# Issuing the two shift-row matmuls behind a pair's second units in a windowed-attention kernel

## Chip, cores and metric

The kernel runs on one core of one Trainium2 chip. The metric is the device time of one execution in microseconds (us). Engines are named as in the profile: PE (TensorE, matmuls), DVE (VectorE), ACT (ScalarE), POOL (GpSimd), SP (the queue that issues the DMAs).

## Reference: what is computed

A group normalisation (32 groups over 384 channels, per image) is followed by shifted window attention with a residual, on 16 images of 56 x 56 tokens. Cut to what matters:

```
x = x + attention(group_norm(x))
# attention: roll by (-3, -3); qkv = x @ w_qkv.T; windows of 7 x 7 = 49 tokens, 12 heads of 32
dots = q @ k.T * 32 ** -0.5 + pos_emb[relative index] + shift masks (last window row, last window column)
out = softmax(dots) @ v; out = out @ w_out.T + b_out; roll back by (3, 3)
```

## Kernel before

**Tiling.** A row is a band of 7 image rows: 8 windows, 392 tokens. There are 128 rows (8 an image), and a row has four pairs of windows. The unit of work is a step: one pair, k = 0 to 7 within a tick of two rows, and p = k % 4 within the row, so steps p = 0, 1, 2, 3 repeat 128 times (512 steps). The four compute engines each run a hand-written instruction stream with a loop over images and, inside, four ticks of eight steps; they meet only at semaphores. Nothing reorders the work: an engine that waits holds up everything written behind it.

**Precision.** Each float32 operand is kept as a high and a low half-precision part, and a product takes three matmuls (high-high, high-low, low-high).

**What PE issues in step t**, in this order (function `step`, from line 1316): `transposed_scores(t - 1)`, `scores(t)`, `transpose_attended(t - 3)`, the first part of the step's units, `attend(t - 2)`, `shift_rows(t)`, the second part, `project_out(t)`, the third part.

**Units** prepare the next row while this one is attended. A q, k or v unit is nine matmuls of about 390 columns (`project_unit`, L1201 and L1205); an x unit transposes a third of the channels of a later row (`x_unit`, four matmuls, L1189). The table FILL spreads them over the four steps of a row:

```
FILL = [([("q", 0)], [("k", 0)], [("q", 1)]),
        ([("k", 1)], [("q", 2), ("x", 0)], [("k", 2), ("x", 1)]),
        ([("v", 0)], [("x", 2)], [("v", 1)]),
        ([("v", 2)], [], [("v", 3)])]
```

So the second part is k0 in step p = 0, q2 and x0 in p = 1, x2 in p = 2 and nothing in p = 3. All units of the program alternate between two PSUM banks (ps_pj): a unit may start when the unit two before it has been taken from its bank. A q, k or v unit is taken in two moves: ACT copies the high part (qk L686, vh L682), then DVE subtracts it for the low part (qk L973, vl L968), and only then is the bank free. An x unit is taken by DVE alone (xn L960).

**Shift rows.** `shift_rows` is two small matmuls (L1257) that turn the row maxima (mt, made by DVE: lg L1008, mx L1024, mw L1030, mt L1041 and L1045) into rows that shift the logits. ACT copies them (tq L762), POOL spreads them over the heads (rb L653), and PE's `transposed_scores` of the next step adds them (L1269). ACT's order in a step is fixed as well:

```
                    shift_rows(t)
...
                        probabilities_high(t - 1)
...
                        x_highs(tk, k)
                        units(tk, k, 1)
                        units(tk, k, 2)
```

That is: tq, then ph (two exponentials, L775), then the high parts of x, and then the high parts of the second and third units. DVE's order is logits, maxima, attended_low (atl L1019), low part of the first unit, `invert` and `normalize` (rv L1049, av L1054), low parts of the second units, the group statistics of a later image (L809), `output` (xb L1063), `split_probabilities` (pl L1069), low parts of the third units. POOL's is rb, its half of pl (L639), the low parts of x (xl L619), the residual (xb L627).

**Exceptions to the common row.** `project_out` (nine matmuls, L1310) has a chunk in steps p = 2, 3, 0 and in p = 1 of every sixteenth row only. The sixth row of an image (but the last) also makes the next image's statistics on DVE and PE (L1177), and the row before it measures more groups. The last image measures none. The last row has no units.

Of the kernel before, what the change touches and what calls it, by code (L numbers as in the profile page):

```python
# [109 lines left out]
def need(eng, sem, value):  # L110

    if isinstance(value, int) and value <= 0:
        return
    eng.wait_ge(sem, value)
# [70 lines left out]
def chunk_at(t):  # L185

    row, p = divmod(t, PAIRS)
    row, part = {2: (row - 1, 0), 3: (row - 1, 1), 0: (row - 2, 2), 1: (row - 2, CHUNKS)}[p]
    if not 0 <= row < ROWS or part == CHUNKS and row % SHARE != SHARE - 1:
        return None  # L190
    return row, part
# [6 lines left out]
def chunks_before(t):  # L198
    return sum(u < t for u in CHUNK_STEPS)
# [22 lines left out]
def step_units(tk, k):  # L222
    first, second, third = ([u for u in part if u[0] != "x" or not tk.last] for part in FILL[k % 4])
    return first, second, [("mean", 0)] * (k == 4 and tk.finishes) + [("var", 0)] * (k == 5 and tk.finishes) + third
# [10 lines left out]
def units_before(tk):  # L235
    return PRO_UNITS + tk.image * IMAGE_UNITS + sum(len(units_in(Tick(tk.image, part))) for part in range(tk.part))


def unit_at(tk, k, kind, i):
    return len(units_in(tk, range(k))) + units_in(tk, [k]).index((kind, i))  # L240
# [20 lines left out]
def build(nc, x, w_qkv, pos, w_out, b_out, const, y):  # L261
# [7 lines left out]
    with ctx:  # L269
# [877 lines left out]
        def _(pe):  # L1147
# [26 lines left out]
            def stat_unit(kind, unit, bank, fz):  # L1174
                bank_free(unit)
                pe.wait_ge(s_fz, fz)
                mm(ps_pj[bank][:, 0:GROUPS], const_of("mean_of", SP_), (red1 if kind == "mean" else red4)[:, :],  # L1177
                   start=True, stop=True).then_inc(s_pj, 1)
# [5 lines left out]
            def x_unit(unit, bank, b, c, loaded):  # L1184

                bank_free(unit)
                pe.wait_ge(s_load[b], loaded)
                for p in range(PAIRS):
                    m = nc.tensor.transpose(ps_pj[bank][:, p * PT:(p + 1) * PT], xs[:, b, p, c * 128:(c + 1) * 128],  # L1189
                                            perm_in[:, 1 if p == PAIRS - 1 else 0, :])  # L1190
                m.then_inc(s_pj, 1)

            def project_unit(unit, bank, kind, i, b, x_ready):
                bank_free(unit)
                pe.wait_ge(s_xh, x_ready)
                pe.wait_ge(s_xl, x_ready)
                for c in range(KC):
                    for n_, (xa, wa) in enumerate(((xh, wh), (xh, wl), (xl, wh))):
                        on = dict(start=c == 0 and n_ == 0, stop=c == KC - 1 and n_ == 2)
                        if kind == "v":  # L1200
                            m = mm(ps_pj[bank][:, 0:C], xa[:, b, c, 2 * i:2 * i + 2, :].rearrange("p w n -> p (w n)"),  # L1201
                                   wa[:, c, 2 * C:3 * C], **on)
                        else:
                            o = (C if kind == "k" else 0) + i * 128
                            m = mm(ps_pj[bank][:, 0:RT].rearrange("p (w n) -> p w n", w=NW), wa[:, c, o:o + 128],  # L1205
                                   xa[:, b, c, :, 0:N], **on)
                m.then_inc(s_pj, 1)
# [11 lines left out]
            def units(tk, k, part):  # L1219

                base, odd, n = units_before(tk), k // 4, tk.n
                for kind, i in step_units(tk, k)[part]:
                    j = unit_at(tk, k, kind, i)
                    if kind == "x":
                        x_unit(base + j + 1, j % 2, odd, i, LOADS * (n + 2))
                    elif kind in STAT_KINDS:
                        stat_unit(kind, base + j + 1, j % 2, FZ * (tk.image + 1) + (2 if kind == "mean" else FZ_MEAN))
                    else:
                        project_unit(base + j + 1, j % 2, kind, i, 1 - odd, 6 * n + 6 + 3 * odd)
# [12 lines left out]
            def scores(t, tk, k):  # L1242
                odd, p, n = k // 4, k % 4, tk.n
                if p == 0:
                    pe.wait_ge(s_stack[odd], STACK * (n + 1))
                need(pe, s_lg, t)
                need(pe, s_tc, t)
                for hh in range(2):
                    m = score_blocks(ps_sa, odd, p, hh, False, start=True, stop=True)
                m.then_inc(s_sa, 1)  # L1250

            def shift_rows(t):

                pe.wait_ge(s_ml, t + 1)
                need(pe, s_tc, t)
                for hh in range(2):
                    m = mm(rows_out[:, hh, :], mt[:, hh, :], eb[:, :], start=True, stop=True)  # L1257
                m.then_inc(s_tp, 1)

            def transposed_scores(t, tk, k):  # L1260

                odd, p = k // 4, k % 4
                pe.wait_ge(s_rb, t + 1)
                need(pe, s_ph, t)
                kind = bias_kind(tk, odd, p)
                for hh in range(2):
                    for w in range(2):
                        rows = slice(w * PAD, (w + 1) * PAD)
                        mm(ps_st[rows, hh, 0:HH * N], bt[:, kind, rows], rb[:, hh, :, :].rearrange("p h n -> p (h n)"),  # L1269
                           start=True, stop=False, skip_group_check=True)  # L1270
                for hh in range(2):
                    m = score_blocks(ps_st, odd, p, hh, True, start=False, stop=True, skip_group_check=True)
                m.then_inc(s_st, 1)
# [14 lines left out]
            def transpose_attended(t):  # L1288
                pe.wait_ge(s_av, t + 1)
                need(pe, s_fin, chunks_before(t + 3))  # L1290
                for c in range(KC):
                    m = nc.tensor.transpose(at_out[:, c, :],  # L1292
                                            av[:, 4 * c:4 * c + 4, :].rearrange("p h d -> p (h d)"), perm_out)
                m.then_inc(s_at, 1)

            def project_out(t):
                if not chunk_at(t):
                    return
                row, part = chunk_at(t)
                pe.wait_ge(s_al, min(t - 2, PAIRS * ROWS))  # L1300
                need(pe, s_fin, chunks_before(t))
                if part == CHUNKS:
                    pe.wait_ge(s_over, row + 1)
                for c in range(KC):
                    if part == CHUNKS:
                        high, low = overh[:, c, :], overl[:, c, :]
                    else:
                        high, low = (a[:, row % 2, c, part * 128:part * 128 + 128] for a in (ath, atl))
                    for n_, (a, w) in enumerate(((high, woh), (high, wol), (low, woh))):
                        m = mm(ps_post[:, 0:C], a, w[:, c, :], start=c == 0 and n_ == 0, stop=c == KC - 1 and n_ == 2)  # L1310
                m.then_inc(s_out, 1)

            def back(tk, k, lag):
                return (tk, k - lag) if k >= lag else (tk.back, k - lag + 8)

            def step(tk):
                for k in range(8):
                    t = 8 * tk.n + k
                    if not (tk.first and k < 1):
                        transposed_scores(t - 1, *back(tk, k, 1))  # L1320
                    scores(t, tk, k)
                    if not (tk.first and k < 3):
                        transpose_attended(t - 3)
                    if not (tk.last and k >= 4):
                        units(tk, k, 0)
                    if not (tk.first and k < 2):
                        attend(t - 2, *back(tk, k, 2))
                    shift_rows(t)
                    if not (tk.last and k >= 4):
                        units(tk, k, 1)  # L1330
                    project_out(t)
                    if not (tk.last and k >= 4):
                        units(tk, k, 2)

            def image(m):
                for part in range(PARTS):
                    step(Tick(m, part))
# [33 lines left out]
```

## Time and profile before

| | |
|---|---|
| time, median of 3 runs | 4250.94 us (4249.82 to 4251.36) |
| profiled execution: time, span | 4250.67 us, 4248.9 us |
| mean granted TensorE clock | 0.996 |
| PE busy | 3998.8 us (94%), 64304 matmuls |
| DVE, ACT, POOL busy | 3676.0 us (87%), 2313.5 us (54%), 2102.1 us (49%) |
| DMA | 131 GB/s on average, 16 engines 48.5% busy with the kernel's own queue |

Busy shares are averages over the whole span. Matmuls are pipelined, so PE at 94% is not PE at its peak, and the time between the starts of two neighbouring groups says more than the duration of one. The time not covered by work of an engine shows in the waits.

### The profile page before, as it was taken

To read this page: it belongs to the slowest core of one execution; us is meant where nothing else is said; L and a number is where in the kernel's file an instruction comes from. 1 tells how busy PE (TensorE), PEld (TensorE's weight loads), DVE (VectorE), ACT (ScalarE), POOL (GpSimd) and SP (SyncE) were. 2 spreads that over 40 slices of the span, in tenths; PEclk is the share of its full clock that TensorE was granted. 3 is DMA by queue.
4 is the path that set the end of the run, shared out by engine and by line. 5 is a ranking of instruction groups with operands and counts; after the bars stand their busy time and mean duration, and the time that the engine had idled before them with its cause. 6 is when DMAs were issued, how large, how long until landed. Compare 5 with 4: busy or idle time off the path is not lost.

```text
span 4248.9 us, 163876 instructions
## 1 busy us (share of the span) xinstructions
PE 3998.8 (94%) x64304; PEld 2757.0 (65%) x64304; DVE 3676.0 (87%) x9291; ACT 2313.5 (54%) x4609; POOL 2102.1 (49%) x1813
## 2 busy tenths in 40 slices
PE   3999999999999999999999999999999999999998
PEld 1666666666666666666666666666666666666665
DVE  6888888888888888888888888888888888888886
ACT  0555555555555555555555555555555555555554
POOL 1445545544554545554455455545545455554554
PEclk9999999999999999999999999999999999999998
DMA  4445455454544554554454554545555545544542
GB/s 125 121 130 144 125 135 143 126 135 131 135 134 132 133 136 128 133 142 122 130 147 125 133 139 128 138 132 132 133 132 137 136 126 135 137 127 130 135 112 80
DMA packets 288056, 555.95 MB, mean 131 GB/s; under 512 B 45793, under 2 KB 197858, under 8 KB 279906
## 3 DMA queue, kind: packets, MB, share of 16 engines
q1 hardware_dynamic: 287298, 545.46, 48.5%
q8 instruction: 522, 8.55, 0.9%
q14 instruction: 236, 1.93, 0.2%
HBM read 237.00 MB, written 77.07 MB: 74 GB/s over the span
## 4 chain that ended last, share of the span: by engine, by line
PE 81%; DVE 9%; ACT 6%; issue 2%; SPq 1%; DMA 0%; POOL 0%; DVEq 0%; ACTq 0%; POOLq 0%
PE ps_pj L1205 23%; PE ps_pj L1201 16%; PE ps_post L1310 14%; PE ps_post L1292 5%; ACT ph L775 4%; PE ps_st L1269 4%; PE ps_sa L1239 3%; PE ps_st L1239 3%; PE ps_pv L1285 3%; PE ps_pv L1284 3%; PE ps_pv L1283 3%; PE ps_pj L1189 2%; ACT qk L686 2%; DVE qk L973 1%; DVE mx L1024 1%
## 5 line engine op out<-in xcount | busy, mean ns | idle before, releaser
L653 POOL TENSOR_TENSOR rb<-tq,cst 128x588 bf16<-128x588 bf16 x512 | 606.4, 1184 | 1851.7 <-ACT tq L762 1851.7
L686 ACT ACTIVATE qk<-ps_pj 128x392 f16<-128x392 f32 x768 | 382.0, 497 | 922.0 <-PE ps_pj L1205 915.8
L1205 PE MATMUL ps_pj<-xh,wh 128*128 128x392 f16 x2304 | 766.9, 333 | 116.5 <-DVE qk L973 105.3
L973 DVE TENSOR_TENSOR qk<-ps_pj,qk 128x392 f16<-128x392 f32 x768 | 434.0, 565 | 395.1 <-ACT qk L686 382.7
L775 ACT ACTIVATE ph<-ps_st,sc 64x588 f16<-64x588 f32 x1024 | 772.2, 754 | 6.4
L1205 PE MATMUL ps_pj<-xh,wl 128*128 128x392 f16 x2304 | 765.3, 332 | 0.0
L1205 PE MATMUL ps_pj<-xl,wh 128*128 128x392 f16 x2304 | 765.1, 332 | 0.0
L639 POOL TENSOR_TENSOR pl<-pf,ph 64x588 f16<-64x588 f32 x512 | 650.4, 1270 | 152.0 <-POOL rb L653 147.5
L1069 DVE TENSOR_TENSOR pl<-pf,ph 64x588 f16<-64x588 f32 x512 | 547.9, 1070 | 1.0 <-ACT ph L775 0.9
L1283 PE MATMUL ps_pv<-vh,ph 128*128 128x33 f16 x6144 | 516.6, 177 | 0.2 <-DVE pl L1069 0.2
L1285 PE MATMUL ps_pv<-vh,pl 128*128 128x33 f16 x6144 | 515.6, 177 | 0.0
L1284 PE MATMUL ps_pv<-vl,ph 128*128 128x32 f16 x6144 | 515.6, 177 | 0.0
L1283 PEld LDWEIGHTS ps_pv<-vh,ph 128*128 128x128 f16 x6144 | 484.5, 96 | 35.9 <-DVE pl L1069 0.7
L1201 PE MATMUL ps_pj<-wh,xh 128*128 128x384 f16 x1536 | 500.8, 326 | 1.7 <-DVE qk L973 0.8
L1201 PE MATMUL ps_pj<-wh,xl 128*128 128x384 f16 x1536 | 500.7, 326 | 0.0
L1201 PE MATMUL ps_pj<-wl,xh 128*128 128x384 f16 x1536 | 500.7, 326 | 0.0
L1284 PEld LDWEIGHTS ps_pv<-vl,ph 128*128 128x128 f16 x6144 | 474.6, 96 | 35.2
L682 ACT ACTIVATE vh<-ps_pj 128x384 f16<-128x384 f32 x512 | 252.6, 493 | 440.2 <-PE ps_pj L1201 440.1
L619 POOL TENSOR_TENSOR xl<-xn,xh 128x392 f16<-128x392 f32 x384 | 447.6, 1179 | 89.5 <-ACT xh L692 69.7
L768 ACT ACTIVATE pf<-ps_st,sc 128x588 f32<-128x588 f32 x512 | 384.8, 752 | 174.6 <-PE ps_st L1239 147.5
L1285 PEld LDWEIGHTS ps_pv<-vh,pl 128*128 128x128 f16 x6144 | 473.8, 96 | 0.0
L1024 DVE TENSOR_REDUCE mx<-lg 128x12 f32<-128x588 f32 x512 | 392.3, 766 | 17.6
(115 smaller groups left out, 8536.2 us busy)
## 6 DMA issues: line engine op xcount, KB each, us to landing
stack<-qk SPq DMA_DIRECT2D x1536, 147.0 KB
sx<-in_x SPq DMA_DIRECT2D x66, 1176.0 KB, 8.1
xb<-in_x SPq DMA_DIRECT2D x368, 192.0 KB
out<-xb SPq DMA_DIRECT2D x368, 192.0 KB
xs<-in_x SPq DMA_DIRECT2D x384, 84.0 KB
xs<-in_x SPq DMA_DIRECT2D x384, 63.0 KB
xs<-in_x SPq DMA_DIRECT2D x128, 66.0 KB
xs<-in_x SPq DMA_DIRECT2D x128, 49.5 KB
```

The costliest lines, as they stand in the source:

```text
L639: nc.gpsimd.tensor_tensor(pl[PAD:, :, PAD:PAD + N], pf[PAD:, :, :], ph[PAD:, :, PAD:PAD + N], ALU.subtract).then_inc(s_pl[1], 1)
L653: nc.gpsimd.tensor_tensor(rb[:, :, :, :], tq[:, :, :].unsqueeze(2).broadcast_to([128, 2, HH, N]), const_of("own_head").unsqueeze(1).unsque ...
L686: nc.scalar.activation(qk[:, K_HIGH if kind == "k" else Q_HIGH, i, :], ps_pj[bank][:, 0:RT], ACT.Copy).then_inc(s_hi, 1)
L775: e = nc.scalar.activation(ph[rows, :, w * PAD:w * PAD + N].rearrange("p (a h) n -> p a h n", a=2), ps_st[rows, :, 0:HH * N].rearrange("p ...
L973: nc.vector.tensor_tensor(qk[:, lp, i, :], ps_pj[bank][:, 0:RT], qk[:, hp, i, :], ALU.subtract).then_inc(s_pjr, 1)
L1069: nc.vector.tensor_tensor(pl[0:PAD, :, 0:N], pf[0:PAD, :, :], ph[0:PAD, :, 0:N], ALU.subtract).then_inc(s_pl[0], 1)
L1201: m = mm(ps_pj[bank][:, 0:C], xa[:, b, c, 2 * i:2 * i + 2, :].rearrange("p w n -> p (w n)"), wa[:, c, 2 * C:3 * C], **on)
L1205: m = mm(ps_pj[bank][:, 0:RT].rearrange("p (w n) -> p w n", w=NW), wa[:, c, o:o + 128], xa[:, b, c, :, 0:N], **on)
L1283: mm(out, ph[:, h, :], v, start=True, stop=False, skip_group_check=True)
L1284: mm(out[:, 0:HD], ph[:, h, :], vl[:, odd, p, h, :], start=False, stop=False, skip_group_check=True)
L1285: m = mm(out, pl[:, h, :], v, start=False, stop=True, skip_group_check=True)
L1310: m = mm(ps_post[:, 0:C], a, w[:, c, :], start=c == 0 and n_ == 0, stop=c == KC - 1 and n_ == 2)
```

## The change

PE's stream alone is edited. In every step, `shift_rows(t)` is issued behind the second part of the units instead of in front of it. No instruction is added or removed, and the streams of DVE, ACT, POOL and SP are the same as before.

```
@@ -1325,9 +1325,9 @@
                         units(tk, k, 0)
                     if not (tk.first and k < 2):
                         attend(t - 2, *back(tk, k, 2))
-                    shift_rows(t)
                     if not (tk.last and k >= 4):
                         units(tk, k, 1)
+                    shift_rows(t)
                     project_out(t)
                     if not (tk.last and k >= 4):
                         units(tk, k, 2)
```

PE in a step p = 1, before the change, from the end of `attend` to the first matmuls of the third part (L1257 the shift rows, L1205 the nine matmuls of q2 and then of k2, L1189 x0; lines left out repeat the pattern):

```order
L1285 MATMUL ps_pv<-vh,pl 128x33
L1257 MATMUL ps_sa<-eb,mt 128x49 [waits shift_rows_taken,maxima_low]
L1257 MATMUL ps_sa<-eb,mt 128x49
L1205 MATMUL ps_pj<-xh,wh 128x392 [waits x_low_written,x_high_written,unit_taken]
L1205 MATMUL ps_pj<-xh,wl 128x392
...
L1189 MATMUL ps_pj<-cst,xs 128x98 [waits row_loaded_even,unit_taken]
L1189 MATMUL ps_pj<-cst,xs 128x98 x3
L1205 MATMUL ps_pj<-xh,wh 128x392 [waits x_low_written,x_high_written,unit_taken]
```

The same place after the change:

```order
L1285 MATMUL ps_pv<-vh,pl 128x33
L1205 MATMUL ps_pj<-xh,wh 128x392 [waits x_low_written,x_high_written,unit_taken]
L1205 MATMUL ps_pj<-xh,wl 128x392
...
L1189 MATMUL ps_pj<-cst,xs 128x98 [waits row_loaded_even,unit_taken]
L1189 MATMUL ps_pj<-cst,xs 128x98 x3
L1257 MATMUL ps_sa<-eb,mt 128x49 [waits shift_rows_taken,maxima_low]
L1257 MATMUL ps_sa<-eb,mt 128x49
L1205 MATMUL ps_pj<-xh,wh 128x392 [waits x_low_written,x_high_written,unit_taken]
```

The shift rows have moved past q2 and x0 and now stand directly in front of k2, which waits for q2 to be taken from its bank.

PE in a step p = 2 after the change (L1189 is x2, L1310 the first matmul of `project_out`):

```order
L1285 MATMUL ps_pv<-vh,pl 128x33
L1189 MATMUL ps_pj<-cst,xs 128x98 [waits row_loaded_even,unit_taken]
L1189 MATMUL ps_pj<-cst,xs 128x98 x3
L1257 MATMUL ps_sa<-eb,mt 128x49 [waits shift_rows_taken,maxima_low]
L1257 MATMUL ps_sa<-eb,mt 128x49
L1310 MATMUL ps_post<-woh,ath 128x384 [waits output_made,attended_low]
```

Here they moved past the four matmuls of x2. In p = 0 they move past the nine of k0, and in p = 3 nothing moves.

On ACT, whose stream is the same before and after, the shift rows' copy stands ahead of the high part of the second unit, here in p = 1:

```order
L762 ACTIVATE tq<-ps_sa 128x98 [waits shift_rows_spread,shift_rows_in_psum]
L775 ACTIVATE ph<-ps_st,sc 64x12x49 [waits attended_in_psum]
L775 ACTIVATE ph<-ps_st,sc 64x12x49
L686 ACTIVATE qk<-ps_pj 128x392 [waits stacks_filled_even,unit_in_psum] x2
```

The last row is the high parts of q2 and k2. Nothing moved in it; what moved is the matmul that its first row waits for.

## Rows read from the trace of the kernel before

**Rows 1.** The page, part 1: busy time, share of the span, instructions.
```profile
PE 3998.8 (94%) x64304; PEld 2757.0 (65%) x64304; DVE 3676.0 (87%) x9291; ACT 2313.5 (54%) x4609; POOL 2102.1 (49%) x1813
```
**Rows 2.** The page, part 4: the chain that ended last, by engine.
```profile
PE 81%; DVE 9%; ACT 6%; issue 2%; SPq 1%; DMA 0%; POOL 0%; DVEq 0%; ACTq 0%; POOLq 0%
```
**Rows 3.** Waits, whole span: who waited for whom, us, times, longest.
```profile
DVE qk L973 <- ACT qk L686: 382.7, 394, 6.8
PE ps_pj L1205 <- DVE qk L973: 105.3, 105, 1.0
PE ps_sa L1257 <- DVE mt L1045: 25.0, 37, 1.1
```
**Rows 4.** Timeline, PE, step p = 1: start us, us, instruction, [idle before].
```profile
2018.99 0.21 PE L1257 MATMUL ps_sa<-eb,mt 128*128 128x49 bf16 x2
2019.04 0.33 PE L1205 MATMUL ps_pj<-xh,wh 128*128 128x392 f16 x1
...
2020.57 0.50 PE L1189 MATMUL ps_pj<-cst,xs 98*128 98x98 f32 x4
2022.08 0.34 PE L1205 MATMUL ps_pj<-xh,wh 128*128 128x392 f16 x1 [1.01 <-DVE qk L973]
```
**Rows 5.** Timeline, ACT, the same step.
```profile
2019.23 0.25 ACT L762 ACTIVATE tq<-ps_sa 128x98 bf16<-128x98 f32 x1 [0.46 <-PE ps_sa L1257]
2019.38 1.52 ACT L775 ACTIVATE ph<-ps_st,sc 64x588 f16<-64x588 f32 x2
2020.93 0.50 ACT L686 ACTIVATE qk<-ps_pj 128x392 f16<-128x392 f32 x1
```
**Rows 6.** Timeline, DVE: low parts of k0, k1 and q2 (p = 0, 1, 1).
```profile
2012.97 0.57 DVE L973 TENSOR_TENSOR qk<-ps_pj,qk 128x392 f16<-128x392 f32 x1 [1.35 <-ACT qk L686]
...
2018.82 0.56 DVE L973 TENSOR_TENSOR qk<-ps_pj,qk 128x392 f16<-128x392 f32 x1
...
2021.46 0.57 DVE L973 TENSOR_TENSOR qk<-ps_pj,qk 128x392 f16<-128x392 f32 x1 [1.35 <-ACT qk L686]
```
**Rows 7.** Timeline, PE and POOL, step p = 0: shift rows, rb, project_out, q1.
```profile
2010.50 0.21 PE L1257 MATMUL ps_sa<-eb,mt 128*128 128x49 bf16 x2
...
2011.07 1.18 POOL L653 TENSOR_TENSOR rb<-tq,cst 128x588 bf16<-128x588 bf16 x1 [3.15 <-ACT tq L762]
...
2012.08 0.32 PE L1310 MATMUL ps_post<-woh,ath 128*128 128x384 f16 x1
...
2013.54 0.33 PE L1205 MATMUL ps_pj<-xh,wh 128*128 128x392 f16 x1
```
**Rows 8.** Timeline, DVE, a fifth row of an image: low parts of k0, k1.
```profile
496.89 0.57 DVE L973 TENSOR_TENSOR qk<-ps_pj,qk 128x392 f16<-128x392 f32 x1 [1.35 <-ACT qk L686]
...
503.19 0.55 DVE L973 TENSOR_TENSOR qk<-ps_pj,qk 128x392 f16<-128x392 f32 x1
```
**Rows 9.** Timeline, all engines, steps p = 2 and 3: x2, project_out, residual, maxima, shift rows.
```profile
2027.87 0.54 PE L1189 MATMUL ps_pj<-cst,xs 98*128 98x98 f32 x4
...
2028.25 0.33 PE L1310 MATMUL ps_post<-woh,ath 128*128 128x384 f16 x1
...
2033.35 0.99 POOL L627 TENSOR_TENSOR xb<-xb,bout 128x384 f32<-128x384 f32 x1
...
2034.00 0.38 DVE L1030 TENSOR_TENSOR mw<-mx,cst 128x24 f32<-128x24 f32 x1
...
2034.62 0.19 DVE L1045 TENSOR_TENSOR mt<-mw,mt 128x24 bf16<-128x24 f32 x1
...
2035.04 0.21 PE L1257 MATMUL ps_sa<-eb,mt 128*128 128x49 bf16 x2
```
**Rows 10.** Timeline, PE: the longest idle time inside the first steps.
```profile
109.22 0.49 PE L1239 MATMUL ps_sa<-stack 96*49 96x49 f16 x24 [3.38 <-DMA stack<-qk]
```
**Rows 11.** Stretches, PE: from:to, length, PE busy (x), granted clock, DMA share, GB/s.
```profile
109.00:114.00 5.00, 4.78 (x42) 0.66 0.27 91
4205.00:4210.00 5.00, 2.60 (x58) 0.59 0.03 9
```

More of the change, by code:

```diff
@@ L1327, in step @@
                         attend(t - 2, *back(tk, k, 2))
-                    shift_rows(t)
                     if not (tk.last and k >= 4):
                         units(tk, k, 1)
+                    shift_rows(t)
                     project_out(t)
```

## Prediction

> **What bounds the kernel now.** I read the page first: PE is busy 94% of the span, DVE 87% [rows 1], and the chain that ended last lies on PE for 81% [rows 2]. So what lengthens PE's stream lengthens the kernel. Then the waits: inside the loop PE waits in one place that matters, at a unit that needs a q unit's low part, 105 times for 105.3 us, that is 1.0 us each; it waits for the row maxima for only 25.0 us in all. Behind the first stands another: DVE waits 382.7 us for ACT's high parts [rows 3]. Last, the timeline of one common row of four steps, for the chain behind the 1.0 us.
>
> The reader is to see this in step p = 1. The shift rows start at 2018.99, q2 at 2019.04, x0 at 2020.57, and k2 not before 2022.08, with 1.01 us of idle PE ahead of it [rows 4]. k2 uses the bank of q2. q2 was finished at 2020.57, but ACT was in its queue: tq at 2019.23, ph from 2019.38 for 1.52 us, and only then q2's high part, 2020.93 to 2021.43 [rows 5]. DVE's low part runs 2021.46 to 2022.03 [rows 6], and PE goes on 0.05 us later. All of it hangs on the start S of the shift rows: tq at S + 0.24, high part at S + 1.94, low part at S + 2.47, bank free for k2 at S + 3.09. Before, 1.58 us of that (shift rows and q2) and then x0 ran beside it. The change issues q2 and x0 ahead of S, so nothing is left to run beside it.
>
> **The change, part by part.** No instruction is added or removed; the two matmuls cost the same wherever they stand.
>
> *Step p = 1, q2 and x0.* The nine matmuls of q2 take 2020.57 - 2019.04 = 1.53 us [rows 4]; x0 takes 0.38, the distance from x2's start to the next group, 2028.25 - 2027.87 [rows 9]. S comes 1.91 us later, and k2 still starts at S + 3.09. The price is 1.91 us a row. The idle time before k2 grows from 1.0 to 3.04 us (S + 0.05 to S + 3.09).
>
> *Step p = 0, k0.* Behind the shift rows come project_out and q1 [rows 7], which need neither tq nor k0's bank: PE loses nothing here at once. rb is wanted by the next step's transposed scores. They come behind q1, at 2013.54 + 1.53 = 2015.07, which is 3.04 us behind the new S of 2012.03; rb starts 0.57 us behind S and takes 1.18 [rows 7], so it has 1.3 us in hand. But S is 1.53 us later (k0), and with it k0's high part on ACT and its low part on DVE, from 2012.97 to 2014.50. DVE has no gap between that and k1's low part, 5.85 us later at 2018.82 [rows 6]; so k1's low part goes to 2020.35, ends at 2020.91, and its bank is free at 2020.96. x0 needs that bank, and would now start at 2018.99 + 1.53 = 2020.52. It waits 0.44 us: price 0.44 a row, on top of the 1.91, since S follows x0.
>
> *Step p = 2, x2.* S is 0.38 us later [rows 9]. PE is not held here: project_out and v1 stand behind. POOL's queue (rb, pl, xl, residual) is held 0.38. In step p = 3 DVE's mw took 0.38 us and ended at 2034.38, just behind the end of POOL's residual (2033.35 + 0.99 = 2034.34); mt followed and ended at 2034.81, and the shift rows at 2035.04 had 0.18 us in hand [rows 9]. If mw waits for the residual's end, mt ends 0.38 later, at 2035.19, and the shift rows start 0.05 behind it at 2035.24: 0.20 us a row. If it doesn't, 0. I take 0.20, because the end of mw fits. The Trainium skill, page "SBUF — State Buffer", section "SBUF: two separate sides", says that DVE with two SBUF inputs and GpSimd hold their shared port pair exclusively for a whole instruction; by that rule this term is 0.20, by a mere sharing of bandwidth nearly 0 and the total 25 us lower.
>
> *Step p = 3.* Nothing moves.
>
> *Rows that differ.* In the fifth row of an image DVE takes 503.19 - 496.89 = 6.30 us instead of 5.85 [rows 8], so x0 waits about 0.4 longer: 2.95. In the sixth (the statistics) k0's late low part meets other DVE work; my estimate lies between the common price and the fifth row's: 2.8. In seven rows project_out (1.46 us [rows 7]) stands in p = 1. There k2 started at S + 0.05 + 1.53 + 0.38 + 1.46 = S + 3.42 before and starts 3.09 behind an S that is 2.35 later now: 2.02, with p = 3 2.2. In the last image DVE measures no groups and should have the 0.44 us to spare: 2.1. Of 127 rows with units: 83 x (1.91 + 0.44 + 0.20 = 2.55) = 212; 15 x 2.95 = 44; 15 x 2.8 = 42; 7 x 2.2 = 15; 7 x 2.1 = 15. Together 328 us of waits.
>
> *The clock.* The granted clock is 0.996 over the span, so PE runs at 2.4 GHz nearly throughout, with gaps of 1.0 us. It did fall elsewhere. After 3.38 us of idle PE [rows 10] the next 5 us were granted 0.66, a part at 1.2 GHz, which took 0.34 x 5.00 = 1.70 us of full-speed clock. At the end, where there are no units and PE is busy 2.60 of 5.00 us, it was granted 0.59 with no such long gap [rows 11]. A gap of 3.04 us with an idle 0.44 before x0 is near the first, in every row but the seven with project_out in p = 1 and the last image's last: 119 times. The bounds are 0 and 1.70 us each. I take 1.4, because the gap is nearest to the one of 3.38 and some of the slow time will lie on idle time, where it costs nothing: 119 x 1.4 = 167 us.
>
> Sum, against the profiled execution's 4250.67 us (0.3 under the median, so no correction): 4250.7 + 328 + 167 = 4745.7, **4745 us**, 11.6% slower.
>
> **Rivals.**
>
> 1. *The clock stays up.* For it: the gap is shorter than 3.38 us, and a fall was seen only behind that one or where PE was idle half the time. Against it: both those stretches, and that the idle time here is nearly as long. 4250.7 + 328 = 4579 us. The Trainium skill's page "TensorE: Matmul & The Clock Gate", section "HAM oscillation — how this bites in real kernels", speaks of idle time that takes the clock down and warns of gaps; read strictly, this gap is still one that it allows, and by that rule this rival holds.
>
> 2. *The clock falls twice a row or stays low longer.* At the end of the program it was at 0.59 for 5 us, so it does not always return at once [rows 11]. 328 + 2 x 167 more: 4913 us. Against it: the other three steps of a row are as dense as before.
>
> 3. *Only k2's wait grows*, by 1.91; DVE and POOL catch up elsewhere, and the clock stays: 4250.7 + 127 x 1.91 = 4493 us. It needs slack on DVE between k0 and k1, where I see none [rows 6].
>
> 4. *The other side: faster.* The second units give DVE 0.4 to 1.5 us more time for the maxima, so that PE no longer waits for mt in the steps where a unit has moved. That is worth at most the 25.0 us of [rows 3]: 4226 us. It decides where the work issued behind the shift rows covers the 3.09 us from S to the low part of the moved unit. In p = 0 project_out and q1 do (1.46 and more from 2012.08 to 2013.54 [rows 7]) and k0's bank isn't wanted at once; in p = 1 nothing stands there, so it fails where the 105 waits are.
>
> That ACT could take q2 before ph is excluded: its stream is in program order and unchanged.
>
> **How the numbers follow.** Forecast (waits and one clock fall a row) 0.66; clock stays up 0.19; more falls 0.08; only k2's wait 0.05; faster or no change 0.02. The predicted time is that of the first, whose own range is 4680 to 4800 (0.9 to 1.7 us a fall, with or without the 25 us of p = 3). The range reaches down to rival 1, since a fifth of the chance lies there: 4565 to 4810, and leaves out rivals 2 to 4. A measurement of this kernel can tell about 0.2% (8.5 us) from no change. Faster 0.01, same 0.01, slower 0.98.
>
> **What would show it.** In the profile after: k2's wait for DVE's qk near 3.0 us each instead of 1.0, some 120 times, so 350 us or more; a new wait of x0 (PE L1189) for DVE's qk, about 0.4 us some 110 times; ACT's q2 high part still 1.94 us behind the start of the shift rows; mw in p = 3 longer than 0.38 and a short wait of the shift rows there; a mean granted clock near 0.95 instead of 0.996 (119 x 1.70 = 202 us of 4745), and near 1.0 if rival 1 holds. A common row should become 4.0 us longer (2.6 under rival 1). The prediction is wrong in its main part if k2's wait stays near 1 us, or if the time is below 4490.

## Result and profile after

| | before | after |
|---|---|---|
| time, median | 4250.42 us (4249.82 to 4251.36, 4 runs) | 4708.85 us (4706.66 to 4709.72, 4 runs) |
| profiled span | 4248.9 us | 4707.0 us |
| mean granted clock | 0.996 | 0.967 |

The ratio is 1.1078 (95% interval 1.1064 to 1.1092): 458 us slower, where 495 were forecast.

The page of the changed kernel, parts 1 and 4; its lines answer to [rows 1] and [rows 2]:

```profile
PE 4127.4 (88%) x64304; PEld 2829.9 (60%) x64304; DVE 3729.1 (79%) x9291; ACT 2302.7 (49%) x4609; POOL 2101.2 (45%) x1813
...
PE 51%; DVE 29%; ACT 12%; issue 7%; SPq 0%; DMA 0%; DVEq 0%; POOL 0%; ACTq 0%; POOLq 0%
```

PE's busy time rose by 129 us with the same instructions, so some of them ran more slowly, and its share fell from 94% to 88%: it also waits more. The chain now passes through DVE for 29% and ACT for 12%. The waits of the changed kernel, who for whom, us in total, times, longest; they answer to [rows 3]:

```profile
DVE qk L973 <- ACT qk L686: 777.8, 387, 6.8
...
PE ps_pj L1205 <- DVE qk L973: 329.9, 127, 2.9
...
PE ps_post L1292 <- DVE xb L1063: 63.8, 104, 1.1
PE ps_pj L1177 <- DVE qk L973: 43.2, 15, 2.9
```

The second row went from 105.3 to 329.9 us. The third is as good as new (0.8 us, once, before). The last is the same wait as the second in the sixth rows of the images, where a statistics matmul stands in k2's place (14.5 us before); together the two are 373 us. The timeline of the changed kernel says where, in a common row of windows. PE in steps p = 0 and 1 (start us, us, instruction, [idle before]):

```profile
2165.22 0.21 PE L1257 MATMUL ps_sa<-eb,mt 128*128 128x49 bf16 x2
...
2169.96 0.52 PE L1292 MATMUL ps_post<-cst,av 128*128 128x128 f32 x3 [0.53 <-DVE xb L1063]
...
2172.76 0.33 PE L1205 MATMUL ps_pj<-xh,wh 128*128 128x392 f16 x1
...
2174.29 0.50 PE L1189 MATMUL ps_pj<-cst,xs 98*128 98x98 f32 x4
2174.63 0.21 PE L1257 MATMUL ps_sa<-eb,mt 128*128 128x49 bf16 x2
2177.72 0.34 PE L1205 MATMUL ps_pj<-xh,wh 128*128 128x392 f16 x1 [2.88 <-DVE qk L973]
```

ACT in step p = 1 of the same row, which answers to [rows 5]:

```profile
2174.88 0.25 ACT L762 ACTIVATE tq<-ps_sa 128x98 bf16<-128x98 f32 x1 [2.33 <-PE ps_sa L1257]
2175.03 1.52 ACT L775 ACTIVATE ph<-ps_st,sc 64x588 f16<-64x588 f32 x2
2176.57 0.50 ACT L686 ACTIVATE qk<-ps_pj 128x392 f16<-128x392 f32 x1
```

With S = 2174.63 the high part of q2 starts at S + 1.94 and k2 at S + 3.09, as before the change [rows 4]; what ran beside that stretch now runs ahead of it. DVE in the same two steps, which answers to [rows 6]:

```profile
2167.69 0.57 DVE L973 TENSOR_TENSOR qk<-ps_pj,qk 128x392 f16<-128x392 f32 x1 [2.88 <-ACT qk L686]
2168.18 1.12 DVE L809 BATCH_NORM_STATS2 st<-sx 112x6 f32<-112x84 f32 x7
2169.21 0.60 DVE L1063 SCALAR_TENSOR_TENSOR xb<-ps_post,sc,xb 128x384 f32<-128x384 f32 x1
...
2173.39 0.55 DVE L973 TENSOR_TENSOR qk<-ps_pj,qk 128x392 f16<-128x392 f32 x1
```

k0's low part is at S + 2.47 again (2167.69 - 2165.22). Behind it come the statistics and then the output, which ends at 2169.81; PE's transposes of p = 1 wait for that (2169.96). k1's low part ends at 2173.94, 0.35 us before x0 starts, so x0 does not wait: the new wait of x0 that the prediction named as a sign is absent. From x0 to S are 2174.63 - 2174.29 = 0.34 us.

Step p = 3 of the same row, POOL's residual, DVE's maxima and PE's shift rows, each row from its engine's timeline; they answer to [rows 9]:

```profile
2189.38 1.00 POOL L627 TENSOR_TENSOR xb<-xb,bout 128x384 f32<-128x384 f32 x1
...
2189.76 0.66 DVE L1030 TENSOR_TENSOR mw<-mx,cst 128x24 f32<-128x24 f32 x1
...
2190.66 0.19 DVE L1045 TENSOR_TENSOR mt<-mw,mt 128x24 bf16<-128x24 f32 x1
...
2190.91 0.22 PE L1257 MATMUL ps_sa<-eb,mt 128*128 128x49 bf16 x2
```

mw ends at 2190.42, 0.04 us behind the residual's end at 2190.38, as it did before; it took 0.66 us instead of 0.38, and the shift rows start 0.06 us behind mt. In the list of waits most of this stands at project_out behind them, which waits for DVE's next output, atl (L1310 for L1019, 23.9 us instead of 5.4); the shift rows' own wait for mt fell from 25.0 to 17.7 us.

The clock: two stretches of 10 us from the same place of two neighbouring rows (from:to, length, PE busy, granted clock, DMA share, GB/s).

```profile
2174.60:2184.60 10.00, 7.12 (x129) 1.00 0.73 192
2209.10:2219.10 10.00, 7.11 (x105) 0.83 0.22 55
```

Both hold the same gap (2.88 and 2.89 us). Around the second the granted clock was at 1.2 GHz for a while and at 2.4 GHz for the rest: 0.17 x 10.00 = 1.7 us of full-speed clock were lost (a "fall" below), and PE got through 105 matmuls instead of 129.

From the starts of tq, row by row: of the 82 common rows 28 are 2.68 us longer than before, and 54 are 4.20 us longer on average. In all 82 k2 starts 3.09 or 3.10 us behind S, and the clock fell in just those 54. So the waits cost 2.68 us a row (2.55 forecast), and a fall of the clock another 1.52 (1.4 forecast), but only in two rows of three.

### The profile page after: what moved, and what is told of

Read it like the earlier page. It is cut to its first block, busy times and chain, and to the rows that moved or that the text cites. A ratio compares the mean times of both kernels' runs of the same rounds, so it can differ in the third digit from the quotient of the medians.

```text
span 4707.0 us, 163876 instructions
## 1 busy us (share of the span) xinstructions
PE 4127.4 (88%) x64304; PEld 2829.9 (60%) x64304; DVE 3729.1 (79%) x9291; ACT 2302.7 (49%) x4609; POOL 2101.2 (45%) x1813
## 4 chain that ended last, share of the span: by engine, by line
PE 51%; DVE 29%; ACT 12%; issue 7%; SPq 0%; DMA 0%; DVEq 0%; POOL 0%; ACTq 0%; POOLq 0%
PE ps_pj L1205 23%; ACT ph L775 8%; PE ps_post L1310 6%; PE ps_pj L1201 6%; DVE pl L1069 4%; DVE mx L1024 4%; ACT qk L686 3%; DVE st L809 3%; DVE lg L1008 3%; PE ps_post L1292 3%; DVE xn L960 2%; PE ps_pj L1189 2%; DVE qk L973 2%; PE ps_pv L1285 2%; DVE mw L1030 2%
## 5 line engine op out<-in xcount | busy, mean ns | idle before, releaser
L1205 PE MATMUL ps_pj<-xh,wh 128*128 128x392 f16 x2304 | 793.7, 344 | 337.7 <-DVE qk L973 329.9
L1205 PE MATMUL ps_pj<-xl,wh 128*128 128x392 f16 x2304 | 797.1, 346 | 0.0
L1205 PE MATMUL ps_pj<-xh,wl 128*128 128x392 f16 x2304 | 795.6, 345 | 0.0
L1069 DVE TENSOR_TENSOR pl<-pf,ph 64x588 f16<-64x588 f32 x512 | 584.8, 1142 | 1.1 <-ACT ph L775 1.1
L1205 PEld LDWEIGHTS ps_pj<-xh,wh 128*128 128x128 f16 x2304 | 226.0, 98 | 499.1 <-DVE qk L973 345.8
L762 ACT ACTIVATE tq<-ps_sa 128x98 bf16<-128x98 f32 x512 | 129.8, 254 | 765.7 <-PE ps_sa L1257 765.7
```

What stands on the lines that cost most here:

```text
L1069: nc.vector.tensor_tensor(pl[0:PAD, :, 0:N], pf[0:PAD, :, :], ph[0:PAD, :, 0:N], ALU.subtract).then_inc(s_pl[0], 1)
```

## Experiments

Ten kernels were run beside the kernel before, whose median in those runs was 4251.0 to 4251.3 us.

### The parts of the change, one at a time

The swap in one step of the row only; with (0,) and (2,) in place of (1,) for the others:

```
+                    early = k % 4 in (1,)
+                    if early and not (tk.last and k >= 4):
+                        units(tk, k, 1)
                     shift_rows(t)
-                    if not (tk.last and k >= 4):
+                    if not early and not (tk.last and k >= 4):
                         units(tk, k, 1)
```

**p = 1 alone.** 

> The swap in step p = 1 alone (q2 and x0 ahead of the shift rows), p = 0 and 2 as before. Theory (ACT's queue: tq, ph, then q2's high part, all tied to the start S of the shift rows): S is 1.91 us later, k2 waits 2.9 us for its bank, no wait of transpose_attended for the output, no k0 effect: 127 x 1.91 = 243 us of waits, and the clock falls about as often as in the full change, some 115 us: about 4610 us. Rival (the cost comes from k0's late low part in p = 0): under 100 us more than before, below 4350 us.

Measured: 4630.98 us, ratio 1.0888 (1.0873 to 1.0902). Rows without a fall of the clock are 1.87 us longer (1.91 expected), which is q2's 1.53 us and the 0.34 of x0. The mean clock is 0.954, lower than in the full change, and this is the 20 us above the expectation. The falls are hardly more frequent (57 of the 82 common rows instead of 54), but some last twice as long: 16 of the 57 rows are about 4.5 us longer than before. Two stretches of 12 us from S, one with a short and one with a long fall:

```profile
1585.60:1597.60 12.00, 9.12 (x132) 0.86 0.21 46
1549.30:1561.30 12.00, 9.12 (x126) 0.72 0.53 127
```

The first lost 0.14 x 12.00 = 1.7 us of full-speed clock, the second 0.28 x 12.00 = 3.4. In the full change only three common rows were hit like this. The rival is out.

**p = 0 alone.** 

> The swap in step p = 0 alone (k0 ahead of the shift rows). Theory: k0's low part is 1.53 us late, DVE's chain up to mt of step p = 1 is about 1.4 us late, transpose_attended of p = 1 waits 0.5 us for the output, and the shift rows of p = 1 wait for mt: S there about 1.0 us later, k2 3.09 behind it, so 1.0 x 127 = 122 us and few clock falls: about 4372 us. Rival a (p = 1 holds the whole price): 4250 us. Rival b (only the 0.52 us wait for the output bank reaches the path): 4316 us.

Measured: 4385.83 us, ratio 1.0317 (1.0303 to 1.0331), clock 0.996 as before. A common row is 0.98 us longer. PE's waits in this kernel:

```profile
PE ps_pj L1205 <- DVE qk L973: 121.3, 120, 1.3
PE ps_post L1292 <- DVE xb L1063: 63.9, 104, 1.1
PE ps_sa L1257 <- DVE mt L1045: 54.6, 147, 1.5
```

k0's late low part reaches PE through the output bank (second row) and through the maxima of p = 1 (third). Both rivals are out.

**p = 2 alone.** 

> The swap in step p = 2 alone (x2 ahead of the shift rows). Theory (POOL's queue is 0.38 us later, and mw of p = 3 waits for the end of POOL's residual, so that mt comes 0.25 us late for the shift rows): 127 x 0.25 = 32 us: 4282 us, and mw in p = 3 0.65 us instead of 0.38. Rival (DVE does not wait for POOL): 4250 us and mw unchanged.

Measured: 4283.29 us, ratio 1.0074 (1.0061 to 1.0086); a common row is 0.24 us longer. DVE and POOL in p = 3, each row from its engine's timeline:

```profile
1725.12 0.65 DVE L1030 TENSOR_TENSOR mw<-mx,cst 128x24 f32<-128x24 f32 x1
...
1724.73 1.00 POOL L627 TENSOR_TENSOR xb<-xb,bout 128x384 f32<-128x384 f32 x1
```

mw ends at 1725.77, the residual at 1725.73. 0.38 us on POOL, which is busy half of its time, cost 32 us of the kernel.

The three parts alone come to 380 + 135 + 32 = 547 us, the whole to 458. The rows without a fall show the same: 1.87 + 0.98 + 0.24 = 3.09 against 2.68. The waits of p = 0 and p = 1 overlap: once q2 and x0 stand ahead of the shift rows, these no longer meet a late mt (54.6 us of waits for mt with p = 0 alone, 17.7 in the full change).

### What the clock costs

```
+                    if k % 4 == 1 and not (tk.last and k >= 4):
+                        need(pe, s_av, t - 1)
+                        for _ in range(14):
+                            mm(ps_pv[:, 0:C], wh[:, 0, 0:128], wh[:, 0, 0:C], start=True, stop=True)
```

> The full change, and in every step p = 1 behind the shift rows 14 extra matmuls of 384 columns (weights times weights) into the bank of the attended values, which is free there; they add work whose result nothing reads. At 0.163 us each they take 2.3 us, inside the 2.9 us that PE waits for q2's bank. Theory (beside the waits the change pays for falls of the TensorE clock behind the long gap): the clock stays at 2.4 GHz and the time comes to what the waits alone cost, 4709 - 120 = about 4590 us, granted clock over 0.99. Rival (no part of the price is the clock's): 4709 us or more.

Measured: 4599.18 us, ratio 1.0821 (1.0805 to 1.0838), clock 0.998. The extra work made the kernel 110 us faster than the plain change. The common rows are now nearly all alike, 2.68 us longer than before, the length of those without a fall. So the price splits into about 345 us of waits and 110 to 115 of clock (this kernel pays some 5 us itself, in the seven rows where project_out already filled the gap).

### The place of q2's high part

The full change, and on ACT:

```
                    if not (tk.last and k >= 4):
                        units(tk, k, 0)
+                    if not (tk.last and k >= 4):
+                        units(tk, k, 1)
                    shift_rows(t)
...
                        x_highs(tk, k)
-                        units(tk, k, 1)
                        units(tk, k, 2)
```

> The full change on PE, and on ACT the same move: the high part of the second unit (k0, q2) is copied ahead of tq and ph instead of behind them. Theory (the price is the place of q2's high part behind tq and ph): q2's high part starts 0.2 us behind the end of q2, its low part ends 2.83 us behind the start of q2, and k2 starts 0.2 us earlier than before the change; the 0.25 us of p = 3 stay; no clock falls: 4240 to 4275 us, k2's wait about 1 us. Rival (the late shift rows themselves cost, through rb, transposed scores or the late ph): clearly over 4300 us.

Measured: 4272.68 us, ratio 1.0051 (1.0036 to 1.0066). ACT now copies the high part before tq and ph, here in a row with project_out in p = 1 (start us, us, instruction; every line number behind the edit is one higher in this kernel):

```profile
1704.47 0.50 ACT L686 ACTIVATE qk<-ps_pj 128x392 f16<-128x392 f32 x1 [1.94 <-PE ps_pj L1206]
1704.86 0.25 ACT L763 ACTIVATE tq<-ps_sa 128x98 bf16<-128x98 f32 x1
1705.01 1.52 ACT L776 ACTIVATE ph<-ps_st,sc 64x588 f16<-64x588 f32 x2
```

and PE's waits are

```profile
PE ps_pj L1206 <- DVE qk L974: 83.8, 105, 0.8
```

PE's stream is that of the full change, shift rows as late, and 436 of the 458 us are gone. So it was neither the late tq, rb nor ph that cost, but that the high parts of k0 and q2 stood behind them. The 0.2 us that k2 gains and the 0.24 of p = 3 cancel, as expected; a common row is 0.03 us longer than before. Most of the 22 us that remain lie in the sixth rows, which are 1.06 us longer each (16 us in 15 rows). The clock, 0.991, did not stay up there, as had been expected: it fell once in 12 of these 15 rows.

### Which wait passes on k0's lateness

The full change, with DVE's output ahead of the group statistics in p = 0:

```
+                    if k % 4 == 0:
+                        output(t)
                     if tk.measures and k == 0:
...
-                    output(t)
+                    if k % 4:
+                        output(t)
```

> The full change, and on DVE in steps p = 0 the output is written ahead of the group statistics. It frees the bank of transpose_attended of p = 1 about 1.1 us earlier. Theory (k0's late low part holds DVE's whole chain, and x0's bank would hold PE for 0.44 us if the output's bank did not hold it 0.52 earlier): that wait goes, x0 waits for DVE's qk about 0.44 us instead, and the time is 4690 to 4709 us. Rival (the output's bank alone is the price of p = 0): no new wait of x0, 0.52 us a row less, about 4650 us.

Measured: 4695.18 us, ratio 1.1047 (1.1031 to 1.1064). The time lies in the theory's range, but only half for its reason. The wait for the output is gone. DVE's low part of k1, and PE's last matmul of q2, x0 and the shift rows of p = 1 in this kernel, in a row where project_out follows in p = 1, which does not touch these four (L1208, L1192 and L1260 are the old L1205, L1189 and L1257):

```profile
1880.07 0.55 DVE L973 TENSOR_TENSOR qk<-ps_pj,qk 128x392 f16<-128x392 f32 x1
...
1880.23 0.33 PE L1208 MATMUL ps_pj<-xl,wh 128*128 128x392 f16 x1
1880.68 0.56 PE L1192 MATMUL ps_pj<-cst,xs 98*128 98x98 f32 x4
1881.08 0.21 PE L1260 MATMUL ps_sa<-eb,mt 128*128 128x49 bf16 x2
```

x0 would follow at 1880.40 and starts at 1880.68, 0.06 behind the end of k1's low part: 0.28 us, not 0.44. The common rows around it show the same 0.28. Rows without a fall are 2.44 us longer than before instead of 2.68, while the clock falls in more of them (60 of 82, mean 0.962). So the x0 wait exists, at about half the size that was predicted, hidden behind a larger one.

### x0 ahead of q2

```
-        ([("k", 1)], [("q", 2), ("x", 0)], [("k", 2), ("x", 1)]),
+        ([("k", 1)], [("x", 0), ("q", 2)], [("k", 2), ("x", 1)]),
```

**On the kernel before.** 

> The kernel before, with x0 ahead of q2 in the second part of p = 1, so that k2 needs the bank of x0, which DVE takes without ACT, and x1 the bank of q2. Theory (the 1.0 us a row is the place of q2's high part behind ph, and it is hidden once one more unit stands in between): k2's wait goes, some of it comes back because DVE, 87% busy, is late for the maxima of p = 2: 4130 to 4215 us. Rival (DVE's load sets the row's length anyway): 4250 us, with waits for mt in place of those for qk.

Measured: 4203.91 us, ratio 0.9889 (0.9872 to 0.9905), 1.1% faster than the kernel before. The waits of PE: the one for qk fell from 105.3 us, the one for mt rose from 25.0.

```profile
PE ps_sa L1257 <- DVE mt L1045: 43.8, 137, 1.1
PE ps_pj L1205 <- DVE qk L973: 24.0, 48, 1.0
```

**On the full change.** 

> The full change with x0 ahead of q2. Now the shift rows are issued behind both again, q2's low part still ends 3.04 us behind them, but k2 no longer needs it and x1 does. Theory: k2 starts at once, x1 waits about 1.5 us for DVE's qk, x0 about 1.3 us for k1's low part; the sum of the waits is about that of the full change, but no single gap is 3 us long, so that the clock falls less often: 4600 to 4710 us. Rival (the gap ahead of k2 is the whole price): below 4400 us.

Measured: 4570.39 us, ratio 1.0751 (1.0735 to 1.0767), clock 0.994. PE's waits:

```profile
PE ps_pj L1205 <- DVE qk L973: 162.0, 157, 2.7
PE ps_pj L1189 <- DVE qk L973: 140.1, 104, 1.4
PE ps_post L1292 <- DVE xb L1063: 63.5, 104, 1.1
```

The clock hardly falls any more, though PE still idles long: the one gap has become two. But a common row is 2.10 us longer than before, not 2.68, and the time fell between the two theories. The expectation had the banks wrong. PE in a common row of this kernel (x0, q2, shift rows, x1), and in the second line DVE's low part of k1, from DVE's timeline:

```profile
2102.14 0.54 PE L1189 MATMUL ps_pj<-cst,xs 98*128 98x98 f32 x4
2102.77 0.55 DVE L973 TENSOR_TENSOR qk<-ps_pj,qk 128x392 f16<-128x392 f32 x1
2103.38 0.34 PE L1205 MATMUL ps_pj<-xh,wh 128*128 128x392 f16 x1 [0.70 <-DVE qk L973]
...
2104.92 0.21 PE L1257 MATMUL ps_sa<-eb,mt 128*128 128x49 bf16 x2
...
2108.01 0.56 PE L1189 MATMUL ps_pj<-cst,xs 98*128 98x98 f32 x4 [1.35 <-DVE qk L973]
```

With x0 first it is q2 that needs k1's bank, and x0 waits for nothing. So the shift rows start 1.60 us (q2 and a handoff) behind the end of k1's low part, which is at 2102.77 + 0.55 = 2103.32; in the profile of the full change it is 2174.63 - 2173.94 = 0.69, which is 0.91 less. x1 then starts 3.09 behind S instead of 2179.27 - 2174.63 = 4.64, which is 1.55 earlier. The difference, 0.64 us a row, is about what the row gained (0.58). x1's start in the full change:

```profile
2179.27 0.50 PE L1189 MATMUL ps_pj<-cst,xs 98*128 98x98 f32 x4
```

### The other half of k2's wait

Putting x0 first took back 0.49 us of a common row, not the whole 1.0 of k2's wait, and the wait for mt grew. The next two kernels move the group statistics on DVE, in every step:

```
-                    if not (tk.last and k >= 4):
-                        units(tk, k, 1)
                     if tk.measures and k == 0:
                         dve.wait_ge(s_slab[(n + 1) % 2], 16 * (3 + (n + 1) // 2))
                     if tk.measures and groups_at[k]:
...
                         measured += groups_at[k]
+                    if not (tk.last and k >= 4):
+                        units(tk, k, 1)
```

**With x0 ahead of q2, shift rows where they were.** 

> The kernel before with x0 ahead of q2 (as in e7), and on DVE the group statistics of every step moved ahead of the low parts of its second units, where DVE stands idle for ACT's high part in p = 0 and 1. Theory (e7 gave 0.5 us a row and not 1.0 because DVE was late for the maxima of p = 2 and 3): the other half comes too, the waits for mt fall from 43.8 us to under 20: 4120 to 4180 us. Rival (PE's stream or POOL sets the row's length now): 4204 us as e7.

Measured: 4164.63 us, ratio 0.9797 (0.9783 to 0.9810): 2.0% faster than the kernel before and the fastest kernel here. The wait for mt is 24.2 us (36 times), and a common row is 0.9 us shorter than before.

**Alone.** 

> The kernel before with the group statistics ahead of the second units' low parts, nothing else. Theory (the 1.0 us before k2 is ACT's queue and not DVE's load): k2's wait stays 1.0 us, the time stays within 10 us of 4251 us. Rival (DVE's load is part of that wait): 4200 us or less.

Measured: 4249.21 us, ratio 0.9994 (0.9985 to 1.0003). PE's waits in this kernel:

```profile
PE ps_pj L1205 <- DVE qk L973: 105.9, 105, 1.1
```

So the statistics gain nothing while k2 waits behind ACT's queue, and 39 us once it does not.

## Why the prediction was right, and where it was not

**k2's wait (1.91 us a row).** Right in mechanism and size. p = 1 alone gave 1.87, S + 1.94 and S + 3.09 stand in the profile after, and moving the high parts on ACT took back 436 us. The 0.04 us too much are x0, which takes 0.34 us where it now stands; the 0.38 were read off x2.

**k0's late low part (0.44 us a row).** The mechanism, DVE late by 1.53 us in p = 0, is right; the step that named x0's bank as the place where it reaches PE is wrong. I followed DVE's stream only to k1's low part and passed over the output on the way. `transpose_attended` of p = 1 needs it, because it writes the output's bank, and this comes earlier on PE. That wait is 0.53 us in the profile after, and it hides x0's, which measured by itself is 0.28. I took DVE's 5.85 us between the two low parts as unbroken work; in the row of the profile after they are 5.70 apart. Before, q1's low part between them (2015.80) had still come just behind ACT's high part of q1 (2015.77). That the price came out near, 0.53 for 0.44, is luck: it is the price of another wait.

**POOL and mw in p = 3 (0.20 us a row).** Right: 0.24 in p = 2 alone. The Trainium skill, page "SBUF — State Buffer", section "SBUF: two separate sides", has the pair of ports held exclusively; by that rule the trace agrees, in that mw ended 0.04 us behind POOL's residual before, after and with p = 2 alone.

**Rows that differ.** Fifth rows without a fall 2.97 (2.95), seven rows with project_out 2.41 (2.2), last image 2.2 (2.1). Sixth rows, with the clock held up, 3.03 (2.8). Together the waits were 345 us, the prediction had 328.

**The clock.** Its direction and the price of a fall were right (1.52 for 1.4), its frequency was not: the step "119 times" is the one that failed. The clock fell behind 80 of these 119 gaps, and the cost was 110 to 115 us where 167 were forecast. That is some 54 us too much; the waits, 17 us more than forecast, made up for a part of it, which leaves the 36 us between 4745 and the measured time. One reading behind the step was off as well: the 3.04 us were counted from 0.05 us behind the start of the shift rows, while the 3.38 us of [rows 10] are idle time counted from the end of the work before. Counted like that the gap is 3.09 - 0.21 = 2.88 us, so it was 0.50 us shorter than the 3.38, not 0.34. Why one gap of 2.88 us was followed by a fall and the next was not stays open; how often and for how long it fell differed from kernel to kernel: clock 0.954 with p = 1 alone, 0.962 with the output first, 0.967 in the full change.

**The rivals.** Rival 1 (the clock stays up) had 4579 us; held up by extra work, the kernel took 4599 including some 5 us of that work itself, so its sum was 15 us short and its premise, that the clock stays up by itself, wrong. The Trainium skill's page "TensorE: Matmul & The Clock Gate", section "HAM oscillation — how this bites in real kernels", read strictly, had this gap as one that is allowed; by that reading the measurement disagrees, since two thirds of the gaps of 2.88 us were followed by a fall. Rival 2 came in three common rows only, which are 5.3 us longer than before (with p = 1 alone it came in 16). Rival 3 did not come: k0's lateness by itself cost 135 us with p = 0 alone, so DVE did not catch up. Rival 4, the faster side, failed where it was said to: the wait for mt did fall from 25.0 us, but only to 17.7:

```profile
PE ps_sa L1257 <- DVE mt L1045: 17.7, 22, 1.1
```

## What to carry to other kernels

When a small producer is moved behind larger work on one engine, look on the consuming engine for what stands behind its wait: here a copy of 0.25 us held 1.52 us of exponentials and then the copy that frees a bank, and all of it moved along. Follow the delay through every buffer of the late engine, not only the one that was moved for, and pair a reorder on the producer with the same reorder on the consumer: that took back 436 of the 458 us here, though it left the kernel no faster than before. Where a unit waits for a bank that two engines empty one after the other, it can help to put between them a unit that a single engine empties: x0 ahead of q2 made the kernel before 47 us faster.

## What the hardware showed that was not expected

Adding 14 matmuls a row made the kernel 110 us faster: with them in the wait the mean clock was 0.998 instead of 0.967. The same gap of 2.88 us was followed by a fall in 54 common rows and not in 28, with 1.7 us of full-speed clock lost in nearly all of those where it fell. In the kernel with x0 ahead of q2 on the full change, the idle time was split into waits of 0.70 and 1.35 us, and the clock was 0.994 instead of 0.967.
